# Second LayerNorm and expert gate taken batch by batch: batch 0 ahead on VectorE, batches 1 to 3 in pieces between the expert tiles

## What is computed

```python
x = x + attn(layernorm(x))            # part 1: 8 heads, softmax(q1 k1) - lam * softmax(q2 k2), RMS norm, Wout
h = layernorm(x)                      # the second LayerNorm: mean, variance, scale per token
logits = normalize(h, -1) @ normalize(sim_matrix, 0) - sigmoid(gates)     # 16 experts
gated  = relu(logits); mask = gated > 0, or the two largest where no expert is active
rw     = softmax(where(mask > 0, gated, -inf))                            # the expert weights of a token
q, k, v = [sum_e rw_e * (h @ proj_e) for proj in (q_proj, k_proj, v_proj)]
attn   = softmax(causal(q k^T / 8)) v
out    = x + sum_e rw_e * (attn @ o_proj_e)
```

## Time and profile before

| what | value |
|---|---|
| median of 3 runs | 1398.0 us (1397.77 to 1398.74) |
| the profiled execution | 1397.29 us, of which 1395.1 us lie between its first and last instruction (the span) |
| busy in the span | PE 87%, DVE 86%, ACT 79%, POOL 73% |
| granted TensorE clock, mean | 0.972 of 2.4 GHz |

### The profile page before, as it was taken

One profiled execution on the slowest core, in us unless ns is written; L12 is line 12 of the kernel. 1 busy time (PEld: TensorE's weight loads), 2 busy tenths in 40 slices (PEclk: granted clock), 3 DMA queues, 4 the chain that ended last, 5 costly groups with the idle time before them and its releaser, 6 DMA issues. The chain is left out here.

```text
span 1395.1 us, 24022 instructions
## 1 busy us (share of the span) xinstructions
PE 1208.1 (87%) x8370; PEld 753.3 (54%) x8370; DVE 1196.0 (86%) x1937; ACT 1107.6 (79%) x2031; POOL 1024.6 (73%) x714
## 2 busy tenths in 40 slices
PE   2789999999999999999999999998862599999997
PEld 1344444444454444454444445444431498989897
DVE  5899999999999999999999999999858576767674
ACT  3899999999999999999999999999833455656553
POOL 3689899899989989998998999899942744434320
PEclk9899999999999999999999999999975799999999
DMA  4232111121211112121111212110003876768570
GB/s 112 68 89 66 40 44 52 31 56 44 62 47 39 52 31 57 42 65 51 33 52 31 59 45 61 31 31 1 1 7 55 151 130 120 137 113 146 100 130 10
DMA packets 184598, 86.85 MB, mean 62 GB/s; under 512 B 150176, under 2 KB 166048, under 8 KB 184480
## 3 DMA queue, kind: packets, MB, share of 16 engines
q1 hardware_dynamic: 184480, 85.33, 28.9%
HBM read 7.68 MB, written 2.10 MB: 7 GB/s over the span
## 5 line engine op out<-in xcount | busy, mean ns | idle before, releaser
L490 POOL TENSOR_TENSOR prob<-prob 128x1024 f32<-128x1024 f32 x256 | 604.0, 2359 | 88.4 <-ACT prob L954 72.4
L1245 DVE TENSOR_REDUCE negmax<-score_ps 128x1 f32<-128x1024 f32 x512 | 621.3, 1220 | 35.3 <-PE score_ps L609 26.2
L925 ACT ACTIVATE prob<-score_ps,negmax 128x1024 f32<-128x1024 f32 x512 | 569.8, 1120 | 52.5 <-DVE negmax L1245 47.3
L609 PE MATMUL score_ps<-ka,qa 128*128 128x512 f16 x1024 | 308.3, 383 | 92.6 <-ACT prob L925 81.1
L638 PE MATMUL attn_ps<-probT,v_sb 128*64 128x512 f32 x1024 | 275.9, 618 | 0.8 <-ACT attn_nT L972 0.8
L632 PE MATMUL trans_ps<-ident,prob 128*128 128x128 f32 x2048 | 268.9, 274 | 2.7 <-POOL prob L490 2.7
L632 PEld LDWEIGHTS trans_ps<-ident,prob 128*128 128x128 f32 x2048 | 239.0, 141 | 57.3 <-POOL prob L490 4.0
L557 POOL TENSOR_TENSOR xs<-xnT,rw_all 128x2048 f32<-128x2048 f32 x32 | 117.4, 3671 | 147.3 <-DVE prob L1378 140.5
L488 POOL TENSOR_SCALAR prob<-prob,ccol 128x1024 f32<-128x1024 f32 x192 | 215.0, 1120 | 3.4 <-DVE ccol L1258 3.4
L609 PEld LDWEIGHTS score_ps<-ka,qa 128*128 128x128 f16 x1024 | 88.5, 98 | 211.9 <-ACT prob L925 179.6
L332 DVE COPY probT<-trans_ps 128x512 f32<-128x512 f32 x256 | 174.2, 681 | 3.1 <-PE trans_ps L632 3.1
(11 more groups left out here) (195 smaller groups left out, 1327.9 us busy)
## 6 DMA issues: line engine op xcount, KB each, us to landing
qa<-split SPq DMA_DIRECT2D x256, 64.0 KB, 2.0
ka<-split SPq DMA_DIRECT2D x256, 64.0 KB, 2.0
xg<-xnT SPq DMA_DIRECT2D x16, 512.0 KB, 3.0
resid<-in_L_attn_x SPq DMA_DIRECT2D x4, 512.0 KB, 6.3
wg<-in_L_attn_Wkv SPq DMA_DIRECT2D x32, 64.0 KB, 2.0
out<-prob SPq DMA_DIRECT2D x32, 64.0 KB, 2.5
wg<-in_L_attn_Wq SPq DMA_DIRECT2D x16, 64.0 KB, 1.9
xsT<-prob SPq DMA_TRANSPOSE x64, 4.5
```

The costliest lines, as they stand in the source:

```text
L490: pool.tensor_tensor(prob1[:, n % PROBS, :], prob1[:, n % PROBS, :], prob2[:, n % 4, :], ALU.add).then_inc(mix_ok, 1)
L609: mm = pe.matmul(score_ps[:, sub, kh * HALF:(kh + 1) * HALF], qa[:, par, head * 2 + sub, q0:q0 + P], ka[:, par, head * 2 + sub, kh * HALF: ...
L925: act.activation(prob2[:, n % 4, :] if sub else prob1[:, n % PROBS, :], score_ps[:, sub, :], ACT.Exp, bias=negmax[:, s % 2, sub:sub + 1], ...
L1245: dve.tensor_reduce(negmax[:, s % 2, sub:sub + 1], score_ps[:, sub, :], AX.X, ALU.max, negate=True).then_inc(max_ok, 1)
```

## The change

Batch 0 alone is normed and gated right behind the slots. ACT squares its tokens with the mean as bias and sums in the same instruction; DVE normalises it in eight instructions of 128x128; POOL waits until that is done. ACT and DVE, instead of POOL, finish the last unit of part 1. DVE then makes batch 0's gate in instructions of 128x128, and tile 0 may start when that is done. The drain of halves 30 and 31, the split of the weights (now in five pieces) and the norm and gate of batches 1, 2 and 3 are cut into pieces that stand between the steps of the tile loop: on POOL between the multiplications `xs`, on ACT and DVE in a function `extra(m)`, on PE in a function `between(m, group)`. The loads of the expert matrices are issued earlier, during the last slots. In the diff `LAST_UNIT` is unit 255 and `HALVES` is 32.

```diff
@@ POOL, behind the slots (L528 on of the kernel before)
-            pool.wait_ge(g_mean, 1)
-            pool.wait_ge(mix_ok, STEPS * UNITS)
-            for b in POOL_BATCHES:
-                pool.tensor_tensor(x2c[:, b * NT:(b + 1) * NT, :], resid[:, b * NT:(b + 1) * NT, :],
-                                   tokens(gs[:, 1, b * NT:(b + 1) * NT]), ALU.add).then_inc(g_cP, 1)
...
+            def polished(b, k_out, done):
+                y, v, t = (rows(gs[:, k, :], b) for k in (4, 2, 5))
+                link(pool.tensor_tensor(t, v, y, ALU.mult))
+                link(pool.tensor_tensor(t, t, y, ALU.mult))
+                link(pool.tensor_scalar(t, t, -0.5, 1.5, ALU.mult, ALU.add))
+                link(pool.tensor_tensor(rows(gs[:, k_out, :], b), t, y, ALU.mult), done)
...
+            pool.wait_ge(g_n, NT)
+            weights_low(0)
+            pool.wait_ge(g_sub, 1)
+            weights_low(1)
+            root(HALVES - 2)
+            norm(HALVES - 2)
+            scale_by_experts(0)
+            weights_low(2)
+            ln2_centre(1)
...
+            ln2_scale(1)
+            weights_low(3)
+            root(HALVES - 1)
+            scale_by_experts(1)
+            norm_root(1)
+            pool.wait_ge(cols_ok, HALVES - 1)
+            norm(HALVES - 1)
+            scale_by_experts(2)
+            pool.wait_ge(w_hi, 5)
+            pool.tensor_tensor(eow_split[:, 1, :, :], eow[:, :, :], eow_split[:, 0, :, :], ALU.subtract).then_inc(w_lo, 1)
+            for m in range(3, B * NT):
+                scale_by_experts(m)
+                if m == 3:
+                    gate_logit(1)
+                elif m == 4:
+                    gate_chosen(1)
+                    ln2_centre(2)
+                elif m == 5:
+                    ln2_scale(2)
+                elif m == 6:
+                    gate_kept(1)
+                elif m == 7:
+                    norm_root(2)
+                    gate_weights(1)
+                elif m == 8:
+                    gate_logit(2)
+                elif m == 9:
+                    ln2_centre(3)
...
@@ PE, between groups of experts
+            def between(m, group):
+                if m == 0 and group == 1:
+                    pe.wait_ge(resid_ok, HALVES - 1)
+                    columns(HALVES - 1)
+                    gate_transposes(1)
+                elif m == 0 and group == 3:
+                    project(HALVES - 1)
+                    gate_logits(1)
+                elif m == 2 and group == 3:
+                    pe.wait_ge(resid_ok, HALVES)
+                    pe.wait_ge(g_seen, 2)
+                    gate_transposes(2)
+                elif m == 3 and group == 3:
+                    gate_logits(2)
+                elif m in (9, 10) and group == 3:
+                    gate_transposes(3, (m - 9,))
+                elif m == 11 and group == 3:
+                    gate_logits(3)
@@ ACT, at the end of iteration m
+            def ln2_squares(m0, m1):
+                act.wait_ge(g_mean, m0 // NT + 1)
+                for m in range(m0, m1):
+                    act.activation(x2n[:, m, :], resid[:, m, :], ACT.Square, bias=gs[:, 1, m:m + 1],
+                                   accum_out=gs[:, 7, m:m + 1]).then_inc(g_sq, 1)
...
+            def extra(m):
+                if m == 0:
+                    neg_mean(2)
+                    ln2_squares(2 * NT, 3 * NT)
+                elif m == 1:
+                    gate_exp(1)
+                    seed(2, g_var, 0)
+                elif m == 2:
+                    seed(2, g_nrm, 2)
+                    gate_high(2)
+                elif m == 3:
+                    neg_mean(3)
+                    ln2_squares(3 * NT, 3 * NT + 4)
+                elif m == 4:
+                    ln2_squares(3 * NT + 4, 4 * NT)
+                elif m == 6:
+                    seed(3, g_var, 0)
+                elif m == 7:
+                    gate_exp(2)
+                elif m == 8:
+                    seed(3, g_nrm, 2)
+                elif m in (9, 10):
+                    gate_high(3, (m - 9,))
+                elif m == 15:
+                    gate_exp(3)
@@ DVE, right behind x_low(m + 2) of iteration m
+            def extra(m):
+                if m == 0:
+                    gate_low(1)
+                    last_add(HALVES - 1)
+                elif m == 1:
+                    gate_top(1)
+                    ln2_sum(3)
+                elif m == 3:
+                    gate_low(2)
+                    gate_sums(1)
+                elif m == 4:
+                    gate_read(2)
+                elif m == 6:
+                    gate_top(2)
+                elif m == 9:
+                    gate_sums(2)
+                elif m in (10, 11):
+                    gate_low(3, (m - 10,))
+                elif m == 12:
+                    gate_read(3)
+                elif m == 14:
+                    gate_top(3)
+                elif m == 17:
+                    gate_sums(3)
```

More of the change, by code:

```diff
@@ new lines, in _ @@
+            last_values(2)
+            gate_logits(0)
+            for kt in range(3, 6):
+                last_values(kt)
+            pe.wait_ge(attn_copied, 2 * (HALVES - 1))
+            columns(HALVES - 2)
+            last_values(6)
+            last_values(7)
+            project(HALVES - 2)
+            pe.wait_ge(attnT_ok, HALVES)
+            transposed_rows(attnT_last, trans_ps[:, 1, :])
+            pe.wait_ge(mask_ok, 6)
+            pe.wait_ge(g_seen, 1)
+            def between(m, group):
[16 more added lines that the diff above has]
+                    gate_logits(3)
@@ L794, in tiles2 @@
                         pe.wait_ge(mT_lo, 2 * (m - 3))
-                        if not (first and t == 4):
+                        if m == 4:
+                            pe.wait_ge(w_lo, 5)
+                        else:
                             pe.wait_ge(y_done, m - 4)
@@ L1006, in _, with gate_high, gate_exp @@
-            act.wait_ge(g_v, GEXP)
-            act.activation(gl[:, 8, :, :], gl[:, 7, :, :], ACT.Exp).then_inc(g_exp, 1)
+            def gate_high(b, halves=(0, 1)):
+                if b >= 2:
+                    act.wait_ge(g_lg, b - 1)
+                for half in halves:
+                    act.wait_ge(g_T, 2 * b + half + 1)
+                    act.activation(x2T[:, b % 2, 0, half * HALF:(half + 1) * HALF], gate_ps(b, half), ACT.Copy).then_inc(g_A, 1)
+            def gate_exp(b):
+                cols = slice(b * NT, (b + 1) * NT)
+                act.wait_ge(g_ein, b + 1)
+                act.activation(gl[:, 6, cols, :], gl[:, 7, cols, :], ACT.Exp).then_inc(g_exp, 1)
@@ L1294, in _, with gate_low @@
             slots(ITERS - 1, False, True)
-            def empty_gate(n):
-                for half in range(2):
-                    dve.wait_ge(g_A, 2 * n + half + 1)
+            def gate_low(b, halves=(0, 1)):
+                for half in halves:
+                    dve.wait_ge(g_A, 2 * b + half + 1)
                     cols = slice(half * HALF, (half + 1) * HALF)
-                    dve.tensor_tensor(x2T[:, n % 2, 1, cols], gate_ps(n, half), x2T[:, n % 2, 0, cols],
+                    dve.tensor_tensor(x2T[:, b % 2, 1, cols], gate_ps(b, half), x2T[:, b % 2, 0, cols],
@@ new lines, in gate_top @@
+            def gate_top(b):
+                if b == 0:
+                    dve.tensor_tensor(rows(gl[:, 0, :, :], b), rows(gl[:, 1, :, :], b), per_expert(sgate[:, :]),
+                                      ALU.subtract).then_inc(g_sub, 1)
+                dve.wait_ge(g_sub, b + 1)
+                for t in range(b * NT, (b + 1) * NT):
+                    dve.max(out=top8[:, t, :], in_=gl[:, 0, t, :]).then_inc(g_top, 1)
+                dve.wait_ge(g_top, tops(b) + NT)
+                for t in range(b * NT, (b + 1) * NT):
+                    dve.max_index(out=top8i[:, t, :], in_max=top8[:, t, :], in_values=gl[:, 0, t, :]).then_inc(g_top, 1)
@@ L1379, in x_low, with gate_sums @@
                                   ALU.subtract).then_inc(xs_lo, 1)
-            for m in range(X_AHEAD):
-                x_low(m, m % 2)
+            def gate_sums(b):
+                dve.wait_ge(g_kept, b)
+                link(dve.tensor_reduce(per_tile(0, b), rows(gl[:, 1, :, :], b), AX.X, ALU.add), g_v)
+                dve.reciprocal(per_tile(1, b), per_tile(0, b)).then_inc(g_rec, 1)
+            ln2_variance()
+            ln2_root()
+            ln2_normed()
+            norm_squares()
+            gate_low(0)
+            norm_root()
+            gate_read(0)
+            last_stat(HALVES - 2)
+            gate_top(0)
+            last_root(HALVES - 2)
+            gate_chosen(0)
+            gate_weights(0)
+            last_add(HALVES - 2)
+            last_stat(HALVES - 1)
+            x_low(0, 0)
+            last_root(HALVES - 1)
+            x_low(1, 1)
+            def extra(m):
+                if m == 0:
+                    gate_low(1)
[14 more added lines that the diff above has]
```

(7 more changed lines are left out.)

528 lines of the change are left out of this document (330 added, 198 removed).

## The result

The changed kernel takes 1402.09 us (median of 5 runs, 1401.55 to 1405.17) against 1398.0: a ratio of 1.0035, 95% interval 1.0021 to 1.0048. It is slower by 4.1 us or 0.3%, more than the 0.2% that the prediction took as what three runs can tell. 1396 and "no measurable change" were forecast, so the forecast missed by 6 us and in its sign; the time lies inside the range. The profiled execution took 1402.09 us, its span is 1400.3.

The account below looks back on a forecast made before the run. Bound: the gate of all four batches before the loop, then PE and an equally long ACT-DVE-PE chain. A lead of 10.9 us less 9.3 lost gave 1395.7, 1396.4 against the median: 1396 us forecast, range 1382 to 1406.

Parts of the forecast that it names:

- POOL's list: POOL's queue from the third weight piece, forecast at 1039.0, to the end of tile 6's multiplication, about 1101.
- the pieces of iteration 3: Between `x_high(5)` and `x_high(6)`: `gate_low(2)` 1.28 and `gate_sums(1)` 0.5 on DVE, mean and squares 1.65 on ACT; 3.4 us added.
- iteration 14: Tile loop with `gate_top(3)` behind `x_low`: forecast to grow by 1.85 us, like iteration 6.
- Batch 0 comes out sooner: After part 1: batch 0's gate weights `rw_all` written at 1034.2 instead of 1079.2, 45 us sooner; bounds 1032 and 1039.
- POOL eats half of it: Iterations up to 4: POOL's work of 48.5, 8.8 and 4.1 us leaves tile 6 only 20 us ahead, at about 1101.
- The gain shrinks before iteration 4: Batch 2's copies, then ACT and DVE pieces, put `x_high(6)` at 1110.4 against 1121.29: lead cut to 10.9 us.
- The pieces are added to a chain without slack: From iteration 4: pieces of 4.1 us on ACT and 6.6 on DVE lengthen the loop; 9.3 us lost after small waits.
- the rival of TensorE's lower clock: TensorE stays at its lower clock into the loop, two tiles from iteration 4 on losing time: 1403 us; chance 0.15.
- one of the prediction's signs of being wrong: In the changed profile: a clock under 0.9 after iteration 4.
- Pieces are hidden: Rival: ACT and DVE pieces after iteration 4 fall into waits, so the 10.9 us stay: 1386, at most 1377; chance 0.30.
- All four batches' gate leaves the path: Rival: first expert matmul at about 1050, loop keeps its length plus some 8 us of PE: 1362 us; chance 0.05.
- GpSimd's 128x128 instructions: Rival: they cost nearer the upper bound, `gate_chosen(1)` 14 instead of 5.1 us, iteration 4 9 us later: 1405; chance 0.13.

Follow-up runs that it names:

- start_order: Changed kernel, but PE multiplies batch 0's gate logits before most last values and ACT scales the second half of expert weights before copying those values: 1398.53 us.
- dve_front_late: Changed kernel, but from iteration 4 on DVE's pieces stand ahead of `x_low` instead of behind it: 1393.5 us, ratio 0.9975 to the kernel before.
- chosen_dve: Changed kernel, but `gate_chosen`, `gate_kept` and `gate_weights` of batch 1 run on DVE instead of POOL: 1404.0 us, ratio 1.0043 to the kernel before.
- top_split: Changed kernel, but `gate_top(3)` is cut into two halves of four tiles, behind `x_low` in iterations 14 and 15: 1404.64 us, ratio 1.0049 to the kernel before.

## Why the prediction was wrong

It had the mechanism and the order of the sizes, and failed in three terms that all lie on the same side: the start of POOL's list (2.8 us late), the pieces of iteration 3 (0.5) and iteration 14, behind whose stall TensorE fell to its lower clock (1.75). That clock it had put at nothing there, and in the drain ahead of POOL's list too. Counted from the end of unit 254:

| step | predicted | measured | runs that tell |
|---|---|---|---|
| `rw_all` of batch 0 written | 22.1 | 24.3 | `start_order` |
| POOL's third weight piece starts | 26.9 | 29.7 | `start_order` |
| POOL's list from there to the end of tile 6 | 61.4 | 62.0 | |
| `x_high(6)` | 98.3 | 101.6 | |
| lost from there to the end | 9.3 | 11.05 | `dve_front_late` |

**Batch 0 comes out sooner: mis-sized by 2.2 us, and the third weight piece by 2.8.** I placed the gate's logits when `x2T` is ready (1026.2). They stand behind two tiles of the last values in PE's queue, and started at 1028.05. The normalising took 2.13, not 1.6. The third piece waits for ACT's scaling, which stands behind the copy of the last values; these wait for POOL's `norm` of half 30 and took 2.99 us at a granted clock of 0.64, 1.94 at 1.00. `start_order` changed only these two queues and returned 3.5 us; 1.5 of the 3.6 by which its third piece is sooner are the clock of the changed kernel's profile.

**POOL eats half of it: right.** 61.4 us predicted (48.5 + 8.8 + 4.1), 1043.45 to 1105.40 measured. The wait for `gate_top(1)` was 4.15 (4.1 predicted). That the sum fits so well is partly luck, since single terms were off and cancelled: `gate_chosen(1)` took 6.65 and not 5.1, two `xs` that met an `x_low` took 5.66 and 5.75 as the row of 5.59 said, while the others met small instructions of POOL, which then took 2.06 and 2.25 instead of 0.20:

```profile
1047.38 2.06 POOL L583 TENSOR_TENSOR gs<-gs 128x8 f32<-128x8 f32 x1 [0.15 <-ACT gs L1080]
```

`chosen_dve` adds what the prediction did not see: DVE's list was as long in iterations 1 and 2, so POOL's alone was no lever.

**The gain shrinks before iteration 4: right to 0.5 us.** From `x_high(5)` to `x_high(6)` 11.1 were predicted, 11.61 measured.

**The pieces are added to a chain without slack: right, but for one term.** 11.05 measured, 9.3 predicted. Iteration 6 lost 2.27 (1.85 and a seed of 0.45), the squares of iteration 4 2.13 (1.44 and a `gate_read` of 0.3), and so on. Only iteration 14 is off, 3.56 instead of 1.85: there the rival of TensorE's lower clock came true within the forecast's mechanism. The mean granted clock of that iteration was 0.87, one of the prediction's signs of being wrong. I had priced it only for whole tiles in iterations 0 to 3 and not behind a stall of 2 us in the full loop.

So the step that failed is the sum of the lead and the loss: -10.9 + 9.3 became -7.6 + 11.05 = +3.4. Of the 5.0 us between them 2.8 are the late start, 0.5 iteration 3 and 1.75 iteration 14; the median says +4.1. About 3.2 of the 5.0 us are TensorE at its lower level (1.5 in the drain, 31.29 - 29.77 of the third weight piece above; 1.7 in iteration 14), which the prediction put at nothing there. Most of the rest is PE's and ACT's queues behind part 1.

**The rivals.** "Pieces are hidden" was wrong for this kernel and nearly right for its neighbour: DVE idles 1.30 us or more ahead of every `x_low` from tile 1 on, in the changed kernel too, and `dve_front_late` used that. For "All four batches' gate leaves the path" the first expert matmul came early enough (1053.89, near its 1050), but from there to the end the changed kernel took 44.6 us longer than before, not some 8. GpSimd's 128x128 instructions cost 0.40 to 0.67, far from the upper bound.

What stays open: how much of the 4.1 us of the medians is the clock, and what decides whether a stall brings it. It differs from execution to execution (the changed kernel's five runs lie at 1401.6 to 1402.1 and at 1405.1 and 1405.2), and the kernels with halved pieces did not separate it by time.

## What to carry to other kernels

A piece of work woven into a full loop is cheapest in front of the instruction for which its engine waits anyway: here the sixteen instructions of `gate_top(3)` cost 1.9 us behind `x_low` (3.56 with the lower clock that followed) and 0.5 ahead of it (9.93 us from `x_high(16)` to `x_high(17)` in `dve_front_late`, 9.42 before the change). Before moving work from a saturated engine to an idle one, look at what stands behind it in the new queue and who waits for that. When a predicted sum hangs on when an operand is ready, follow the queue of each engine through the whole stretch, lightly loaded ones too.

## What the hardware showed that I had not expected

- Equal stalls of PE in the full loop brought the lower clock or not. Those of 2.12 to 2.18 us behind a whole `gate_top` were followed by a stretch near a granted clock of 0.5 in 6 of 11 cases (iteration 6 in 2 of 6 profiles, iteration 14 in 4 of 5), at about 1.65 us each. The stalls of 0.74 to 1.56 us by halved pieces brought it in none of three kernels, and neither did one of 3.03 us in `top_split`. So the length of the stall alone does not decide it.
- On GpSimd an instruction of 128x128 with one tensor and two scalar operations takes 0.64 to 0.67 us, one with two tensors 0.40 to 0.46.
- An instruction of 8 columns on GpSimd took 2.06 us, not 0.20, when it started while VectorE's subtraction of 128x2048 ran.
- The first eight matmuls of 128x512 took 5.10 to 6.53 us from one execution to the next. They go together with the granted clock from 50 to 56 us, which was 1.00 in the six profiles with 5.43 us or less and 0.57 to 0.69 in the eight with 5.83 or more, and with the end of unit 254 (1011.94 us with 5.10, 1014.05 with 6.53).
